# Attention step in another order: squares, roots as powers on GpSimd, turned rows and normalisation in other slots

## What is computed

```python
def _features(x, omega, quad_nodes, quad_weights):          # for queries and keys, 16 heads of 16
    xn = x / jnp.maximum(jnp.linalg.norm(x, axis=-1, keepdims=True), 1e-12)
    proj = jnp.einsum('bhtd,rhdm->rbhtm', xn, omega)
    arg = jnp.clip(proj * sqrt_2s - s, -20.0, 20.0)
    feat = jnp.exp(arg) / np.sqrt(M) * jnp.sqrt(jnp.maximum(quad_weights, 0.0))
...
def _layernorm(x, axis=-1, eps=1e-05):
    return (x - mean) / jnp.sqrt(var + eps)
```

## Time and profile before

| | us |
|---|---|
| median of 3 runs | 1610.31 (1608.62 to 1610.74) |
| span of the profiled execution | 1609.7 |
| PE busy in it | 1414.2 (88%) |
| DVE, ACT, POOL busy | 918.4, 683.3, 517.3 |

### The profile page before, as it was taken

The page is one execution under the profiler, slowest core; times in us unless marked ns, Lnnn a source line. Parts: engine busy times, 40 slices in busy tenths (PEclk is TensorE's granted clock), DMA queues, the critical chain, the costliest instruction groups (busy, mean ns, idle before and its releaser), DMA issues. The chain is left out here.

```text
span 1609.7 us, 34137 instructions
## 1 busy us (share of the span) xinstructions
PE 1414.2 (88%) x12248; PEld 1219.4 (76%) x12248; DVE 918.4 (57%) x1994; ACT 683.3 (42%) x1260; POOL 517.3 (32%) x395
## 2 busy tenths in 40 slices
PE   6799999759988989899893899899998999999990
PEld 5688888646766767666673788688888999999990
DVE  4766675747576765766664335334435555555544
ACT  2467566423443533435342323222223555555543
POOL 0245444322324334242300002343202444444440
PEclk7799999969999989999896899799998999999995
DMA  6233422120313223132103701224209888888865
GB/s 246 83 130 135 142 82 75 39 80 15 106 41 129 81 76 117 44 112 78 40 15 115 281 27 63 96 97 147 86 27 241 234 237 234 237 233 238 232 164 215
DMA packets 101207, 204.05 MB, mean 127 GB/s; under 512 B 18448, under 2 KB 72720, under 8 KB 94864
## 3 DMA queue, kind: packets, MB, share of 16 engines
q1 hardware_dynamic: 76032, 144.73, 27.5%
q0 software_dynamic: 23088, 54.31, 11.7%
q10 hardware_dynamic: 2016, 4.08, 0.7%
HBM read 144.53 MB, written 58.55 MB: 126 GB/s over the span
## 5 line engine op out<-in xcount | busy, mean ns | idle before, releaser
L2112 PE MATMUL e_ps<-e_xhl,e_whl 128*128 128x256 f32 x1872 | 248.9, 283 | 3.7 <-DMA e_whl<-wlo 3.7
L2112 PEld LDWEIGHTS e_ps<-e_xhl,e_whl 128*128 128x128 f32 x1872 | 233.7, 190 | 4.3 <-issue 4.3
L1703 PE MATMUL d_ps<-d_xhl,d_whl 128*128 128x512 f32 x768 | 195.3, 403 | 7.5 <-DVE d_whl L1773 5.3
L1703 PEld LDWEIGHTS d_ps<-d_xhl,d_whl 128*128 128x128 f32 x768 | 144.8, 194 | 38.5 <-issue 9.6
L2008 POOL DMA_INDIRECT xs<-e_y,e_slot_id x78 | 121.6, 1559 | 82.9 <-ACT e_y L2039 68.2
L1268 ACT ACTIVATE c_qf<-c_cf,fc 128x512 f32<-128x512 f32 x64 | 46.2, 721 | 221.3 <-DVE c_cf L1370 221.3
L382 POOL TENSOR_TENSOR b_hhl<-b_h,b_hhl 128x512 fp32r<-128x512 f32 x64 | 94.5, 1479 | 138.5 <-ACT b_hhl L609 112.2
L2092 PE MATMUL e_ps<-e_whl,e_ghl 128*128 128x256 f32 x936 | 137.7, 282 | 0.5 <-DVE e_ghl L2186 0.5
L2174 DVE TENSOR_TENSOR e_g<-e_ps,e_act_h 128x256 f32<-128x256 f32 x156 | 66.2, 425 | 115.4 <-ACT e_act_h L2053 96.1
L1878 DVE TENSOR_TENSOR d_g<-d_ps,d_act_h 128x512 f32<-128x512 f32 x64 | 44.2, 691 | 139.8 <-PE d_ps L1703 80.5
L2092 PEld LDWEIGHTS e_ps<-e_whl,e_ghl 128*128 128x128 f32 x936 | 120.5, 188 | 0.7 <-ACT e_ghl L2063 0.7
(11 more groups left out here) (304 smaller groups left out, 2647.7 us busy)
## 6 DMA issues: line engine op xcount, KB each, us to landing
e_whl<-wlo SPq DMA_DIRECT2D x39, 1024.0 KB, 5.0
e_whl<-wlo SPq DMA_DIRECT2D x39, 512.0 KB
c_eraw<-in_expert_w POOLq DMA_DIRECT2D x24, 512.0 KB, 4.7
wlo<-c_elo POOLq DMA_DIRECT2D x24, 512.0 KB, 3.0
wall<-in_expert_w SPq DMA_DIRECT2D x8, 1536.0 KB
xg<-b_zeros POOLq DMA_DIRECT2D x13, 780.0 KB, 3.9
e_xr<-xg SPq DMA_DIRECT2D x39, 260.0 KB
x<-rows_out SPq DMA_DIRECT2D x16, 512.0 KB, 3.1
```

Source lines behind the costliest of these rows:

```text
L1703: mm = pe.matmul(ps[:, H + 2 * (m % 2) + w, :], whl[:, wp, e, lo:lo + P], xhl[:, k, xp, kd, :], start=q == 0, stop=q == 3 * KD - 1)
L2112: mm = pe.matmul(ps[:, H + m, w * SLOT:(w + 1) * SLOT], whl[:, k, wp, lo:lo + P], xhl[:, k, xp, kd, :], start=q == 0, stop=q == 3 * KD - 1)
```

## The change

- A constant tile `halves` of -0.5 is set once by POOL at the start of the attention phase.
- The eleven instructions of Newton's method on the 128x128 norms go; DVE keeps the maximum with 1e-24, and POOL raises the result to the power -0.5 in one instruction. The row roots (128x4 in the attention phase, 128x16 twice in `phase_combine`) and the product with the mean go to POOL in the same way. In POOL's step they come last.
- POOL takes three chunks of expert weights ahead of the squares, and the fourth behind the products.
- DVE sums half 0 of the squares in turn 4 at B (before: after C), half 1 in turn 5 at B as before, and takes the maximum after C of turn 5.
- FN 0, 2 and 1 move to turns 6 C, 7 A and 7 C (before: 7 B, 7 C and turn 0 A of the next step); FN 3 stays at turn 0 B. BO 1 moves from turn 6 C to turn 6 A.
- ACT copies the high parts of point A ahead of the exponentials, and normalises in turn 0 of the next step, after context out.
- The bank of a block follows its number over all steps, and ACT's program has step 1 written out ahead of its loop.

The diff, cut to its core:

```diff
-        SLOTS_OF_X = {0: ((A_, "FN", 1), (B_, "FN", 3), (C_, "BO", 2)),
+        SLOTS_OF_X = {0: ((B_, "FN", 3), (C_, "BO", 2)),
...
-                      6: ((C_, "BO", 1),),
-                      7: ((B_, "FN", 0), (C_, "FN", 2))}
+                      6: ((A_, "BO", 1), (C_, "FN", 0)),
+                      7: ((A_, "FN", 2), (C_, "FN", 1))}
...
                 if not isinstance(i, int) or 1 <= i < LAST:
-                    split_expert_weights(i)
+                    split_expert_weights(i, range(EPER - 1))
                 if is_step(i + 1):
...
                         gp.tensor_tensor(sq[:, bb], qk[:, bb], qk[:, bb], ALU.mult).then_inc(s["sq_ready"], 1)
+                    gp.wait_ge(s["norm_ready"], f + 1)
+                    gp.tensor_tensor(nrm[:, 1, :], nrm[:, 0, :], halves[:], ALU.pow).then_inc(s["rnorm_ready"], 1)
                     for c in range(KD):
                         gp.wait_ge(s["rnorm_ready"], f + 1)
...
+                if not isinstance(i, int) or 1 <= i < LAST:
+                    split_expert_weights(i, range(EPER - 1, EPER))
+                if is_step(i - 1):
+                    row_roots(i)
+
+            def row_roots(i):
+                gp.wait_ge(s["var_ready"], i)
+                gp.tensor_tensor(small[:, 3, :], small[:, 2, :], halves[:, 0:BATCH], ALU.pow).then_inc(s["root_own"], 1)
+                gp.wait_ge(s["root_own"], i)
+                gp.tensor_tensor(small[:, 5, :], small[:, 0, :], small[:, 3, :], ALU.mult).then_inc(s["stats_ready"], 1)
...
+                    x_high(i, t, A_)
                     if pair(i, t, 0) is not None:
                         exponentials(*pair(i, t, 0))
-                    x_high(i, t, A_)
...
                         context_out(i, *pair(i, t, 2))
+                    if t == 0 and is_step(i - 2):
+                        normalise(i - 1)
                     x_high(i, t, C_)
...
-                if is_step(i - 1):
+                if isinstance(i, int) and i == STEPS:
                     normalise(i)
...
-            def norm_guess(ch):
+            def norms(ch):
                 ch.wait()
-                ch.link(ve.tensor_scalar(nv, nv, 1e-24, None, ALU.max))
...
+                ve.tensor_scalar(nv, nv, 1e-24, None, ALU.max).then_inc(s["norm_ready"], 1)
+                ch.end()
...
-                ch.link(ve.scalar_tensor_tensor(v, half_, 0.25, v, ALU.mult, ALU.add))
-
-            def row_scales(ch):
-                rsqrt(ch, v, r, t_, smalli[:])
-                ve.tensor_tensor(nb, mean, r, ALU.mult).then_inc(s["stats_ready"], 1)
+                ve.scalar_tensor_tensor(v, half_, 0.25, v, ALU.mult, ALU.add).then_inc(s["var_ready"], 1)
...
                     x_evac(i, t, A_)
-                    if front and t == 6:
-                        norm_newton(norm, False)
...
                     x_evac(i, t, B_)
+                    if front and t == 4:
+                        squares(norm, i + 1, 0)
                     if front and t == 5:
                         squares(norm, i + 1, 1)
-                    if front and t == 6:
-                        norm_newton(norm, True)
-                        norm.end()
...
                     x_evac(i, t, C_)
-                    if front and t == 4:
-                        squares(norm, i + 1, 0)
                     if front and t == 5:
-                        norm_guess(norm)
-                        norm_newton(norm, False)
+                        norms(norm)
...
+        @block.gpsimd
+        def _(gp):
+            for h in range(2):
+                tt = slice(h * HALF * BATCH, (h + 1) * HALF * BATCH)
+                gp.wait_ge(var_ready, h + 1)
+                gp.tensor_tensor(small[:, 3, tt], small[:, 2, tt], halves[:, 0:HALF * BATCH], ALU.pow).then_inc(root_own, 1)
+                gp.wait_ge(root_own, h + 1)
+                gp.tensor_tensor(small[:, 5, tt], small[:, 0, tt], small[:, 3, tt], ALU.mult).then_inc(scales_ready, 1)
...
-                rsqrt(ch, v, r, t_, smalli[:, tt])
-                ve.tensor_tensor(nb, mean, r, ALU.mult).then_inc(scales_ready, 1)
+                ve.scalar_tensor_tensor(v, half, 0.25, v, ALU.mult, ALU.add).then_inc(var_ready, 1)
```

More of the change, by code:

```diff
@@ L901, in phase_mixer, with phase_attention @@
     nc.all_engine_barrier()
-def phase_attention(nc, x2, bqkv, bout, masks, x3, routed_w, wlo, ids, rows_out, x2_stored, x3_stored, early, x0, x0_in, fc):
+def phase_attention(nc, x2, bqkv, bout, masks, x3, routed_w, wlo, ids, rows_out, x2_stored, x3_stored, early, x0, x0_in, fc, halves):
     with ExitStack() as ctx:
@@ L922, in phase_attention @@
         va = sb("va", [P, BATCH, HEADS1, VP])
-        nrm = sb("nrm", [P, 3, BATCH * 2 * HEADS1])
-        nrmi = sb("nrmi", [P, BATCH * 2 * HEADS1], I32)
+        nrm = sb("nrm", [P, 2, BATCH * 2 * HEADS1])
         qkt = sb("qkt", [P, 2, 2 * KD, TOK], F32R)
@@ L939, in phase_attention @@
         small = sb("small", [P, 6, BATCH])
-        smalli = sb("smalli", [P, BATCH], I32)
         eraw = sb("eraw", [P, 2, EC])
@@ L951, in phase_attention @@
                  "score_done", "mask_done", "kt_done", "kr_ready", "pair_done", "state_new", "ot_ready", "xb_ready",
-                 "stats_ready", "out_ready", "stored", "norm_own", "ln_own", "bo_own", "pre_own")
+                 "stats_ready", "out_ready", "stored", "norm_own", "ln_own", "bo_own", "pre_own",
+                 "halves_set", "norm_ready", "var_ready", "root_own")
         s = {n: sem(n) for n in names if n != "stored"}
@@ L1013, in x_bank @@
         def x_bank(i, name, a):
-            position = [(m, b) for _, _, m, b, _, _ in x_events(i)].index((name, a))
-            return X + position % 2
+            at = i if isinstance(i, int) else 2
+            return X + next(n for _, _, m, b, n, _ in x_events(at) if (m, b) == (name, a)) % 2
         def x_at(i, t, point):
@@ L1074, in _, with split_expert_weights @@
         def _(gp):
-            def split_expert_weights(i):
-                for c in range(EPER):
+            def split_expert_weights(i, chunks):
+                for c in chunks:
                     n = (i - 1) * EPER + c
@@ L1107, in body @@
                                              [P, 2 * BATCH, HEADS1 // KD, HD]), ALU.mult).then_inc(s["qn_ready"], 1)
+                if not isinstance(i, int) or 1 <= i < LAST:
[7 more added lines that the diff above has]
+                gp.tensor_tensor(small[:, 5, :], small[:, 0, :], small[:, 3, :], ALU.mult).then_inc(s["stats_ready"], 1)
+            gp.memset(halves[:], -0.5).then_inc(s["halves_set"], 1)
+            gp.wait_ge(s["halves_set"], 1)
             prime(gp, [elo_ready])
@@ L1309, in body @@
                         expert_high(i, t - 1)
-                if is_step(i - 1):
+                if isinstance(i, int) and i == STEPS:
                     normalise(i)
-            everything(act, body)
+            body(-1)
+            body(0)
+            body(1)
+            with act.Fori(2, LAST) as i:
+                body(i)
+            body(LAST)
+            body(STEPS)
         @block.vector
@@ L1381, in new_state @@
                 ve.tensor_tensor(held, ps[:, OB, SU:SU + BATCH * VP], held, ALU.add).then_inc(s["state_new"], 1)
-            nv, nr, nt = nrm[:, 0, :], nrm[:, 1, :], nrm[:, 2, :]
-            NORM_OWN = 3 + 2 + 3 * 3 - 1
+            nv = nrm[:, 0, :]
+            NORM_OWN = 2
             def squares(ch, f, half):
@@ L1390, in squares @@
                                          sq[:, 2 * half:2 * half + 2].rearrange("p b (n d) -> p (b n) d", d=HD), AX.X, ALU.add))
-            def norm_guess(ch):
+            def norms(ch):
                 ch.wait()
-                ch.link(ve.tensor_scalar(nv, nv, 1e-24, None, ALU.max))
[L1395 to L1408, removed]
+                ve.tensor_scalar(nv, nv, 1e-24, None, ALU.max).then_inc(s["norm_ready"], 1)
+                ch.end()
+            mean, half_, v = (small[:, k, :] for k in range(3))
+            LN_OWN = 4 + 3 + 3
             def row_stats(ch, i):
@@ L1465, in body @@
                         row_moments(rows)
-                        row_scales(rows)
             everything(ve, body)
@@ L2188, in _, with phase_combine @@
             in_turns(ve, GROUPS, body)
-def phase_combine(nc, xs, out):
+def phase_combine(nc, xs, out, halves):
     HALF = STEPS // 2
@@ L2204, in phase_combine @@
         small = sb("small", [P, 6, TILES])
-        smalli = sb("smalli", [P, TILES], I32)
         x_in = [sem(f"x_in{k}") for k in range(STEPS)]
-        own, scales_ready, by_act, by_dve, stored = (sem(n) for n in ("own", "scales_ready", "by_act", "by_dve", "stored"))
+        own, var_ready, root_own, scales_ready, by_act, by_dve, stored = (sem(n) for n in ("own", "var_ready", "root_own", "scales_ready", "by_act", "by_dve", "stored"))
         block = ctx.enter_context(nc.Block())
@@ L2254, in scales @@
                 tt = slice(h * HALF * BATCH, (h + 1) * HALF * BATCH)
```

(11 more changed lines are left out.)

3 lines of the change are left out of this document (1 added, 2 removed).

## The result

The changed kernel takes 1710.21 us (median of 4 runs, 1708.46 to 1713.6) against 1610.53 for the kernel before: a ratio of 1.062 (95% interval 1.060 to 1.063). It is slower by 99.7 us, where 70 less were forecast and 1524 to 1580 us was the range. The profiled execution has a span of 1708.6 us, 98.9 over that of the kernel before.

What follows compares the result with a forecast made beforehand. PE was taken as the bound in turns 1 to 4, DVE past that. Steps falling from 65.8 to 56.1 us save 58.1; with the other phases 70.6 off span 1609.7 gives 1539.1, median 1540, range 1524 to 1580.

Steps and rivals of the forecast that it cites:

- (3): The 128x128 power on POOL: taken as 2.6 us, between a lower end of 0.3 and an upper end of 7.8.
- dear power: Rival: the power on POOL takes 4 to 8.8 us; 1566 us at a power of 5.2; chance 0.16.
- (4): The path to block FN0 that the power joins: PE waits P - 1.45 there, 1.2 us a step.
- P: Time of the 128x128 power on POOL, taken as 2.6 us.
- slower: Rival: the power is a software routine of over 70 ns a column, beyond 8.8 us; 1634 us at 12; chance 0.08.
- (1): Squares on POOL: with the fourth chunk behind the products, DVE's wait of 5.39 us goes; the chunk's move costs nothing.
- (2): Newton's method leaves DVE: 3.5 us a step for the norms and 2.3 for the row scales.
- (5): The order past FN0: the next step's 2.53 us wait goes, and PE is the bound everywhere but at FN0.
- cheap power: Rival: the power takes under 1.45 us, PE doesn't wait at FN0; steps 54.5 us, 1526 us; chance 0.18.
- starved hand-overs: Rival: the clip, exponentials, FN3, state chain on DVE and ACT starves PE, 3 us a step; 1560 us; chance 0.09.
- (6): PE's clock: short half-speed dips cost 1.7 us each; 0.9 us a step kept, a dip every second step.
- The small roots: Row roots on POOL: 0.9 us replaces 2.3 after the last step; in combine roots become 1.1 us, 1.8 gained.

Runs made afterwards that it cites:

- the run with the product: The changed kernel with the 128x128 power on POOL replaced by a product of the same tiles: 1538.14 us, ratio 0.955 to the kernel before.
- the run with half of the columns: The changed kernel with the power on columns 0 to 63 only and a product on columns 64 to 127: 1630.79 us, ratio 1.011.
- the two halves: The changed kernel with norms' roots by Newton's method on VectorE in two 64-column halves, products by halves, last phase as before: 1547.27 us, ratio 0.968.

## Why the prediction was wrong, point by point

**(3) The power's price** is the step that failed, and the only one that did so with weight. It was sized at 2.6 us, with 7.8 as the upper end. It measures 20.81 us: eight times the one, 2.7 times the other; its 160 ns a column are 84 times a multiplication's 1.9. The error was to build a price from operations of a known rate (a root as eleven of them, a power as three times that), when no row showed a function of this kind on this engine; the range closed at 1580 us, below even the 1599 of that upper end. The rule of the Trainium skill (GPSIMD Engine Reference, Performance pitfalls for Q7 kernels), 4 cycles an element for a dependent chain of additions or products, pointed the right way and gave an estimated 4.7 us: taken with eleven links it is too low as well, since 160 ns a column are an estimated 190 cycles at the page's 1.2 GHz. That "every POOL row here runs at 1.9 to 2.3 ns a column" was the argument against a dear power; it held for the rows shown, all of them products or differences (another in the trace, L382, takes 1479 ns for 512 columns, 2.9 each), and said nothing of a function. What was missing was a wider top: no row of a function spoke against the rival on the other side, and it got a chance of 0.08.

**(4) The path** held. The text said that PE waits P - 1.45 us at FN0. With the measured P that is 19.36; the trace has 19.21. With 10.90 (power and product) it is 9.45, measured 9.25, and with 0.46 nothing, as measured. The "slower" rival's own formula gives 54.0 + 19.36 + 3.4 = 76.8 us a step; 76.9 was measured. Its point of decision, P = 8.8, stands against 8.9 by the runs; the prediction's own terms give 9.1 for it (and 1562 us where it has 1563 for P = 4.7), which changes nothing.

**(1) Squares** held in timing: VectorE no longer waits for POOL. The second sum of step 3 in the kernel after starts behind its neighbour without an idle time:

```profile
634.73 1.21 DVE L1409 TENSOR_REDUCE c_nrm<-c_sq 128x64 f32<-128x1024 f32 x1
```

The 10.78 us of idle time that the text gives the moved chunk were misread: they stood ahead of the products. Behind the products and the bias addition POOL was idle for 18.90 us, so the chunk had room there too. The move's worth was not priced apart; the run with it alone shows 1.5 us a step, and there VectorE and ScalarE are late behind it.

**(2) and (5) The new order** held: the forecast for a cheap power was 54.5 us a step and 1526 us, the run with the product has 55.1 and 1538. Of its gain of 84.0 us of span 73.3 came: 3.5 are missing in the six steps, 3.3 ahead of them and 3.9 behind. In the steps PE has a wait of 1.3 us in turn 1, which (5) overlooked: it followed FN 3 only as far as VectorE's evacuation and didn't ask what ScalarE does ahead of its copy. The rival of starved hand-overs named that chain (clip, exponentials, FN3) and overrated it at 3 us. Of the high parts ahead of the exponentials (5) said that "they bring nothing themselves". Whether that held is open: undoing them together with the place of the normalisation costs 17 us, and no run separates the two.

**(6) The clock** held roughly for a short wait: with the product, and a wait of 1.3 us in turn 1, it is 0.99 over six steps, some 0.6 us a step withheld, where 0.9 was kept for a wait of 1.2. After 19.2 us idle PE restarts at the lower level, which goes with the 2.6 us between the 57.7 us that a step takes beside its wait and the 55.1 of the run with the product.

**The small roots**: at the end of the attention phase 1.03 + 0.20 us on POOL replace 2.3 of VectorE, somewhat over the 0.9 assumed. In the last phase 2.92 + 0.22 replace 2.5, where 1.1 was assumed; the gain of 1.8 us came to nothing.

## What to carry to other kernels

An operation that no row prices is not bounded by a guess of its steps: give its range a top at which the sign of the result turns, work out where that is (here 8.9 us, 70 ns a column), and measure one instance before moving work onto it. Ask of a stall that you remove who is late next; the same move was worth 0.5% alone and, with half of the roots behind it, 3.6% once the others were made; and the best version came from naming PE's longest wait after each run. A function that costs by the column can still pay where it is narrow (4 columns here) and lose where it is wide (128).

## What the runs showed of the hardware that was not expected

- A power of fp32 (exponent -0.5) on POOL costs 0.4 us and 160 ns for each column of 128 partitions: 1.03 us for 4 columns, 2.92 for 16, 10.58 for 64, 20.81 for 128. A product takes 0.32 us for 64 columns (the run with half of the columns) and 0.46 for 128.
- VectorE's instructions on 64 columns take 0.225 us (runs from the two halves on) where those on 128 take 0.29: in two halves the work takes 1.5 times as long in all. Whether the halves paid by themselves is not shown: the run that brought them has the ratio of the run without them.
